# Who issues the filter shifts of a pair's second sample: ScalarE in place of SyncE

## The reference

```
x = x + ffn_l(cond_l(x, cond_512, ...), ...)        # l = 0..3

# cond_l: four modulated convolutions of three taps, one after the other
s      = style @ mod_w.T + mod_b                    # per sample and input channel
weight = SCALE * w * s                              # (sample, out, in, 3)
weight = weight * rsqrt(sum(weight ** 2) + EPS)     # demodulation
types  = same, upsample (stride 2 + blur), same, downsample (blur + stride 2)
```

## Time and profile before

| | us |
|---|---|
| median of 3 runs (2082.38 to 2083.69) | 2082.81 |
| the profiled execution, its own time | 2085.02 |
| its span, first to last instruction | 2083.3 |
| PE busy | 1893.3 (91%) |
| PE weight loads busy (beside the matmuls) | 1563.2 (75%) |
| DVE busy | 905.4 (43%) |
| ACT busy | 646.3 (31%) |
| POOL busy | 82.7 (4%) |

### The profile page before, as it was taken

One profiled execution on the slowest core, in us unless ns is written; L12 is line 12 of the kernel. 1 busy time (PEld: TensorE's weight loads), 2 busy tenths in 40 slices (PEclk: granted clock), 3 DMA queues, 4 the chain that ended last, 5 costly groups with the idle time before them and its releaser, 6 DMA issues.

```text
span 2083.3 us, 28693 instructions
## 1 busy us (share of the span) xinstructions
PE 1893.3 (91%) x9806; PEld 1563.2 (75%) x9806; DVE 905.4 (43%) x2634; ACT 646.3 (31%) x1169; POOL 82.7 (4%) x140
## 2 busy tenths in 40 slices
PE   3789999869999999985799999999879999999978
PEld 2567777757888888864688888888767888888855
DVE  5345555644343433344434444444563333333244
ACT  0045555423333333314322232332153332233200
POOL 0000000000000000000000000000000000000000
PEclk9999999969999999986899999999989999999975
DMA  6256666423223323235222222222233232222226
GB/s 125 56 108 149 148 158 155 104 60 82 69 76 82 83 74 83 58 67 119 59 69 58 70 68 58 70 68 52 86 80 79 68 78 66 70 70 78 58 91 262
DMA packets 248777, 182.99 MB, mean 88 GB/s; under 512 B 197688, under 2 KB 207960, under 8 KB 248734
## 3 DMA queue, kind: packets, MB, share of 16 engines
q1 hardware_dynamic: 242750, 175.07, 33.1%
q0 software_dynamic: 4496, 2.12, 1.0%
q10 hardware_dynamic: 1488, 5.26, 0.8%
HBM read 108.99 MB, written 44.04 MB: 73 GB/s over the span
## 4 chain that ended last, share of the span: by engine, by line
PE 75%; issue 9%; DVE 7%; DMA 4%; SPq 4%; ACT 1%; DVEq 0%; POOL 0%; ACTq 0%; POOLq 0%
PE ps L812 61%; PE ps L1485 4%; PE ps L891 3%; DMA filt<-filt 2%; PE ps L939 2%; DVE w_lo L1240 2%; SPq L1073 1%; DMA out_x<-raw 1%; SPq L1310 1%; PE ps L882 1%; DMA raw<-in_x 1%; PE ps L1353 1%; PE ps L1359 1%; SPq L1306 1%; DVE filt L650 1%
## 5 line engine op out<-in xcount | busy, mean ns | idle before, releaser
L812 PE MATMUL ps<-xp_hi,filt 128*128 128x512 f32 x1024 | 338.9, 413 | 28.1 <-DMA filt<-filt 27.9
L812 PE MATMUL ps<-w_hi,y_hi 128*128 128x512 f32 x768 | 313.6, 408 | 0.0
L812 PE MATMUL ps<-w_hi,y_lo 128*128 128x512 f32 x768 | 306.6, 399 | 0.0
L812 PE MATMUL ps<-w_lo,y_hi 128*128 128x512 f32 x768 | 306.3, 399 | 0.0
L812 PEld LDWEIGHTS ps<-xp_hi,filt 128*128 128x128 f32 x1024 | 192.1, 195 | 71.5 <-DMA filt<-filt 30.3
L639 DVE SCALAR_TENSOR_TENSOR xp_lo<-ps,mods_pair,xp_hi 128x512 fp32r<-128x512 f32 x128 | 96.3, 753 | 268.9 <-ACT xp_hi L391 268.9
L812 PE MATMUL ps<-xp_lo,filt 128*128 128x512 f32 x512 | 205.8, 402 | 0.0
L391 ACT ACTIVATE xp_hi<-ps,mods_pair 128x512 fp32r<-128x512 f32 x128 | 88.4, 691 | 359.4 <-PE ps L812 359.4
L812 PEld LDWEIGHTS ps<-w_lo,y_hi 128*128 128x128 f32 x768 | 146.0, 190 | 35.6
L812 PEld LDWEIGHTS ps<-w_hi,y_hi 128*128 128x128 f32 x768 | 147.7, 192 | 31.5
L812 PEld LDWEIGHTS ps<-w_hi,y_lo 128*128 128x128 f32 x768 | 146.6, 191 | 31.1
(11 more groups left out here) (315 smaller groups left out, 3212.3 us busy)
## 6 DMA issues: line engine op xcount, KB each, us to landing
x_in<-x_state SPq DMA_DIRECT2D x96, 256.0 KB, 3.9
x_res<-x_state SPq DMA_DIRECT2D x48, 512.0 KB, 4.0
x_state<-x_res SPq DMA_DIRECT2D x48, 512.0 KB, 2.9
filt<-filt SPq DMA_DIRECT2D x128, 128.0 KB, 2.7
filt<-filt SPq DMA_DIRECT2D x128, 96.0 KB, 2.4
raw<-in_x SPq DMA_DIRECT2D x16, 512.0 KB, 5.0
x_res<-in_x SPq DMA_DIRECT2D x16, 512.0 KB, 3.9
x_state<-raw SPq DMA_DIRECT2D x16, 512.0 KB, 2.9
```

The costliest lines, as they stand in the source:

```text
L812: ins = nc.tensor.matmul(out, st[x0], mv[x1], start=first and t == 0, stop=last and t == 2, **kw)
```

## The change

The two shift DMAs of sample 1 (and their wait for DVE's low part) leave SP's stream and join ACT's. At the start of a layer they stand behind `act_filter` of pair 0, ahead of gu_hi of pair 1, and behind `act_filter` of pair 1, ahead of the loop. In the loop of layer 0 they stand behind xp_hi of sample 0 and ahead of zt_hi; in layers 1 to 3 behind `act_filter`, ahead of zt_hi (layers 1 and 2) or the end of the step (layer 3). The DMAs, their sizes and semaphores are as before, and SP still issues those of sample 0. In all 128 of the 256 shift DMAs move.

```diff
--- before.py
+++ after.py
@@ -313,14 +313,12 @@
 
             return 32 * (g + 1) if l == 0 else 32 * GROUPS + 64 * (GROUPS * (l - 1) + g + 1)
 
-        def sp_shift_filter(sp, l, k):
-
-
-            for q in range(2):
-                sp.wait_ge(s["dve_k"], smp(l, k, q))
-                t = f(filt[q][:])
-                sp.dma_start(t[0:C, 1:WIN, :, 1, :], t[C:P, 0:WIN - 1, :, 0, :]).then_inc(filt_shifted[q], 16)
-                sp.dma_start(t[C:P, :, :, 1, :], t[0:C, :, :, 0, :]).then_inc(filt_shifted[q], 16)
+        def shift_filter(eng, l, k, q):
+
+            eng.wait_ge(s["dve_k"], smp(l, k, q))
+            t = f(filt[q][:])
+            eng.dma_start(t[0:C, 1:WIN, :, 1, :], t[C:P, 0:WIN - 1, :, 0, :]).then_inc(filt_shifted[q], 16)
+            eng.dma_start(t[C:P, :, :, 1, :], t[0:C, :, :, 0, :]).then_inc(filt_shifted[q], 16)
 
         def sp_step(sp, l, i, j, more, load_next):
             n = 2 * i + j
@@ -332,7 +330,7 @@
             if l == 0 and more and j == 1:
                 load_kernel(sp, i + 1)
             if more:
-                sp_shift_filter(sp, l, n + 2)
+                shift_filter(sp, l, n + 2, 0)
             if not more and j == 1 and l + 1 < LAYERS:
 
                 if l + 1 == 2:
@@ -449,12 +447,15 @@
                 act_filter(act, l, n + 2, j)
             if more:
                 act_first(act, l, n + 2, 0, j)
+            if l == 0 and more:
+                shift_filter(act, l, n + 2, 1)
             if l == 0:
                 act_tail_in(act, l, n)
             if more:
                 act_first(act, l, n + 2, 1, j)
                 if l > 0:
                     act_filter(act, l, n + 2, j)
+                    shift_filter(act, l, n + 2, 1)
             if l in (1, 2):
                 act_tail_in(act, l, n)
             if not more and j == 0 and l + 1 < LAYERS:
@@ -1673,9 +1674,9 @@
             for l in range(LAYERS):
                 if l > 0:
                     sp_load_x(sp, l, 0)
-                sp_shift_filter(sp, l, 0)
+                shift_filter(sp, l, 0, 0)
                 sp_load_x(sp, l, 1)
-                sp_shift_filter(sp, l, 1)
+                shift_filter(sp, l, 1, 0)
                 sp_load_x(sp, l, 2)
                 if l == 0:
                     load_kernel(sp, 0)
@@ -1725,6 +1726,7 @@
                 for q in range(2):
                     act_first(act, l, 0, q, 0)
                 act_filter(act, l, 0, 0)
+                shift_filter(act, l, 0, 1)
                 act_filter_in(act, l, 1, 1)
                 act_split_x(act, l, 1, 1)
                 act_halves(act, l, 1, 1)
@@ -1733,6 +1735,7 @@
                 for q in range(2):
                     act_first(act, l, 1, q, 1)
                 act_filter(act, l, 1, 1)
+                shift_filter(act, l, 1, 1)
                 with act.Fori(0, GROUPS - 1) as i:
                     for j in range(2):
                         act_step(act, l, i, j, True, True)
```

## The result

| | before | after |
|---|---|---|
| median, us | 2082.81 | 2103.15 (4 runs, 2101.58 to 2104.36) |
| the profiled execution, its own time | 2085.02 | 2102.81 |
| its span | 2083.3 | 2101.1 |
| PE's mean granted clock | 0.938 | 0.936 |

The ratio of after to before is 1.0097 with a 95% interval of 1.0079 to 1.0114: the change makes the kernel about 1% slower. The two profiled executions differ by 17.8 us, the medians by 20.3 us, because the profiled execution of before lay 2.2 us above its median.

The account below looks back on a forecast made before the run. PE bounds the kernel, busy 1893.3 of 2083.3 us, so only its 190 us of idling could change. The terms 3.8 - 0.5 + 4.0 + 8.4 + 1.0 + 3.0 = 19.7 us gave 2102.5 us, range 2084 to 2112.

Parts of the forecast that it names:

- PE doesn't wait for sample 1: All filter waits stand before sample 0's convolution, so the change speeds up a transfer that is already early.
- Pair 0 of a layer, 3 x 1.27 us: Layers 1 to 3: ACT's two issues put gu_hi of pair 1 1.27 us later, uncovered; 3.8 us.
- Start of layer 0, -0.5 us: Pair 1's x load is issued two issues sooner, so PE's x_lo wait shrinks; -0.5 us, between -1.3 and +1.3.
- Pair 1, 4 x 1.0 us: Each layer's start: sample 1's packets run beside sample 0's awaited second DMA; 1.0 us each, 4.0 in all.
- Odd pairs, 7 x 1.2 us: Layer 0's loop, pairs 3 to 15: moved DMAs can overtake SP's backlog and be served before sample 0's; 8.4 us.
- zt_hi in odd pairs, covered by the filter wait: Layer 0's loop: zt_hi comes at most 1.3 us later, covered by the filter wait, so nothing is paid.
- Even pairs, 7 x 0.15 us: Layer 0's loop, pairs 2 to 14: ACT's issues delay xp_hi of sample 1 by 0.15 us each; 1.0 us.
- Clock, two stretches, 3.0 us: Layer 0's odd pairs: longer waits bring two low-clock stretches of 1.5 us each; 3.0 us (0 to 9.0).
- rival 1: Full turn-taking: sample 0 pays 1.5 us in all 11 places, six waits drop the clock; 29.8 us, 2112.6; chance 0.15.
- Loops of layers 1 to 3, nothing: Sample 0's shift has 2.3 us of cover against at most 1.5, and zt_hi's delay is covered; nothing paid.
- Rival 2: The two queues run side by side for nothing; only 4.3 us stay, 2087.1 us; chance 0.15.
- rival 3: Queues share freely and low clock falls into idling at eight layer-start waits; 7.7 us faster, 2075.1; chance 0.07.

Follow-up runs that it names:

- the experiment: The changed kernel with only the loops of layers 1 to 3 issuing sample 1's shifts on ACT, SP issuing all others: 2082.07 us, ratio 1.0001 to the kernel before.

## Why the prediction came out

The total was met (2102.5 forecast, 2103.15 measured), in part by luck: errors of up to 2.9 us in single terms cancelled, and the sum, which was built from a profile, is 1.8 us above the difference of the profiles and 0.6 below that of the medians. Step by step:

- **PE doesn't wait for sample 1.** Right: after the change too, no convolution of sample 1 has a filter wait, so nothing could be gained.
- **Pair 0 of a layer, 3 x 1.27 us.** Right in mechanism and size: 1.30 us at gu_lo in layer 1, 1.3 to 1.4 us in each of the four layers, 5.2 us in all waits for gu_lo (5.1 forecast), and the later place on ACT takes it away again.
- **Start of layer 0, -0.5 us.** The wait for x_lo vanished as said. With pair 1's longer wait (+0.9) the start comes out at 0.0, where -0.5 + 1.0 was forecast.
- **Pair 1, 4 x 1.0 us.** Right in mechanism; the four gaps grew by 0.87, 0.74, 0.85 and 0.72, together 3.2 us.
- **Odd pairs, 7 x 1.2 us.** This is the step that failed in its mechanism: "They can overtake the backlog and are served before sample 0's." The packets show that they don't, and giving ACT's queue to sample 0 lost time. What is paid is the sharing behind the backlog: landing later by 1.31, 0.84, 0.54, 1.03, 0.89 and 0.80 us, each of which is what the pair lost to within 0.03 us. With 0.2 for pair 15 that is 5.5 us, not 8.4. The prediction had named the sign that would have spoken for it, a shorter landing of sample 1, and that landing grew instead.
- **zt_hi in odd pairs, covered by the filter wait.** Right, though the view of waits seems to say otherwise. PE now waits 0.36 us more at zt_lo, and just so much less at the filter: gaps grew by 0.95, 0.46, 0.18, 0.65, 0.53 and 0.41 us where the landings grew by the figures above. The first wait of a chain takes from the second, and only the landing counts. For the same reason the filter waits reached 34.2 us and not the 40 that were forecast: 2.2 us of the odd pairs' loss stand at zt_lo, and the rest was never paid.
- **Even pairs, 7 x 0.15 us.** The order was right (the issue starts at 308.81, while xp_hi runs until 309.42), the size half of the truth: 0.31 us, as ACT's second issue took 0.87 us, not 0.65. Six pairs give 1.8 us.
- **Clock, two stretches, 3.0 us.** Three in the loop of layer 0, 4.7 us; a fourth in layer 3's loop (1.6). At the starts of layers the low clock moved about and gave 0.9 back: 2.6 + 2.5 + 0.2 = 5.3 us there, while 3 x 1.3 for gu_lo and 2.3 for the three filter waits would be 6.2. The argument against rival 1 that "the clock did not fall after waits of 2 us" misread the kernel before: it had fallen at pair 3, after 2.03 us. How many stretches would fall was a guess that no row supported.
- **Loops of layers 1 to 3, nothing.** Right, in both profiles and in the experiment, although landings there went from 2.7 to between 3.3 and 3.7 us (4.8 once). The cover of 2.3 us was enough: 1.4 of it are left.

The sum, measured less forecast: -2.9 us in the odd pairs, -0.5 at the start of layer 0, -0.7 at pair 1 of the others, +0.1 at gu_lo, +0.8 in the even pairs, +2.4 for the clock (4.7 + 1.6 - 0.9 against 3.0) and -1.0 at the end: 1.8 less than 19.7, which is the 17.8 but for rounding. Rival 2 (no sharing) falls by the landings, rival 1 (1.5 us in every place, the clock in all six) by their size, rival 3 by the clock at the layer starts, which gave back 0.9 us and not 12, and rival 4 by the wait for gu_lo.

Left open: which part of the hardware holds ACT's DMAs behind SP's backlog. The packets show when they start, not what keeps them. Open too is why the clock fell after a wait of 2.14 us and not after 2.49; in the experiments it fell after 1.89 us (pair 5, with ACT's issue last) and not after 2.85 (pair 11, with sample 0 on ACT). Nor did I settle the low clock at the starts of layers: it differs by some 2 us between profiles even where nothing near it was changed. So the reordered kernel load shows 12.1 us in the six odd pairs and one low-clock stretch of 1.5 us fewer, and 10.7 us in the medians (10 by the ratio).

## What to carry to other kernels

Before moving a DMA to another engine's queue, ask whether anyone waits for it, and who waits for the DMAs that it will now run beside: here a transfer that nobody awaited was started sooner, and the one that PE awaits paid. A late small DMA behind large loads was helped here by issuing it ahead of them on the same queue, not by a second queue. And cover is landing time against start of use: a convolution that starts 0.04 us after a landing has none, even where the view of waits shows no wait.

## What the runs showed of the hardware

- DMAs issued by ACT while SP's queue had a backlog had no packet until the backlog was nearly through: q10 is absent from 326.60 to 329.30 us although ACT issued at 325.94, and again from 319.90 to 321.90 after an issue at 318.90. The two queues were served in about the order of issue, whichever of them was ahead. The median landing of ACT's 128 KB shifts is 3.7 us.
- Where both queues have 256-byte packets at once, both samples' landings grow: in the loops of layers 1 to 3 from 2.7 to 3.3-3.7 us for sample 0. In the even pairs of layer 0, where ACT's first issue comes 0.1 us behind sample 0's second and not ahead of it, sample 0's grows only from 2.6-2.7 to 2.8-2.9.
- ACT's second issue of a pair takes 0.65 us in most places and 0.87 in the even pairs of layer 0; the cause is open. An issue starts while the ACTIVATE ahead of it runs, but the next ACTIVATE waits for it.
- A low-clock stretch costs a convolution 1.55 us. It newly followed three of six filter waits of 2.1 to 3.0 us, and their length alone doesn't say which: in other runs it fell after 1.89 us and stayed high after 2.85.
